# One-hot rows of the sources from TensorE and ScalarE, attention scores from W0 times a, and the batches of the front as straight code

## The reference

```
h = relu(layernorm(x));  hw = h @ W0 + b_w
s_dst = hw @ a[:512];    s_src = hw @ a[512:]
e = leaky_relu(s_dst[dst] + s_src[src] + b_a, 0.2);  w = exp(e)
x = x + segment_sum(w / segment_sum(w, dst)[dst] * hw[src], dst)
h = relu(layernorm(x))
gates = softmax(h @ gate_W + gate_b); top 2 of 4 experts
each expert: 2 times h = relu(mean_of_neighbours(h) @ Wl + bl + h @ Wr)
x = x + sum over the top 2 of gate * expert(h)
```

## Time and profile before

| what | value |
|---|---|
| median of three runs | 859.07 us |
| the profiled execution | 863.82 us, span 862.1 us |
| TensorE, matmuls busy | 752.3 us (87%) |
| VectorE busy | 444.7 us (52%) |
| ScalarE busy | 254.6 us (30%) |
| GpSimd busy | 176.2 us (20%) |
| mean granted TensorE clock | 0.973 |

### The profile page before, as it was taken

How to read it: one execution, slowest core, us unless ns; L and a number is a source line. 1 busy time by engine, 2 the same in 40 slices (tenths; PEclk the granted TensorE clock), 3 DMA queues, 4 the chain that set the end, 5 groups by cost and what they waited for, 6 DMA issues and landing times.

```text
span 862.1 us, 11919 instructions
## 1 busy us (share of the span) xinstructions
PE 752.3 (87%) x3620; PEld 611.0 (71%) x3621; DVE 444.7 (52%) x1088; ACT 254.6 (30%) x516; POOL 176.2 (20%) x160
## 2 busy tenths in 40 slices
PE   1019877499997999998999999989999999999994
PEld 0007655388886888876777777768888888888883
DVE  6999999678876415572263343433223332323230
ACT  0113444555555425141141221312211221212120
POOL 6602433300000001055000000023322332233201
PEclk9999899889997999999999999999999999999997
DMA  4200000011124014769989695369934993449910
GB/s 127 84 0 2 0 0 0 1 59 59 62 84 149 2 49 127 241 195 275 304 285 331 223 348 172 105 197 272 327 94 109 274 330 93 110 108 246 343 22 5
DMA packets 46809, 125.30 MB, mean 145 GB/s; under 512 B 7280, under 2 KB 7412, under 8 KB 46752
## 3 DMA queue, kind: packets, MB, share of 16 engines
q1 hardware_dynamic: 29072, 81.58, 29.0%
q0 software_dynamic: 9232, 26.17, 12.1%
q10 hardware_dynamic: 8448, 16.78, 5.6%
HBM read 72.19 MB, written 53.20 MB: 145 GB/s over the span
## 4 chain that ended last, share of the span: by engine, by line
PE 71%; DVE 18%; DMA 4%; issue 3%; DVEq 1%; ACT 1%; POOL 0%; POOLq 0%; SPq 0%; ACTq 0%
PE ps L1417 15%; PE ps L1419 15%; PE ps L1418 15%; PE ps L1714 6%; PE ps L1713 5%; DVE onehot_g L1025 5%; PE ps L1579 3%; DVE column L1013 3%; PE ps L1580 3%; PE ps L1641 3%; DMA raw<-in_L_gnn_Wr 2%; DVE onehot_p L966 2%; PE ps L1685 1%; PE ps L1724 1%; PE ps L1510 1%
## 5 line engine op out<-in xcount | busy, mean ns | idle before, releaser
L1714 PE MATMUL ps<-slots,CTs 125*128 x230 | 90.9, 395 | 0.0
L1713 PE MATMUL ps<-slots,CTs 125*128 x207 | 81.6, 394 | 0.0
L1345 DVE CAST CTs<-ps 125x512 fp32r<-125x512 f32 (+1 forms) x69 | 37.3, 595 | 85.1 <-PE ps L1641 62.0
L611 POOL DMA_INDIRECT out<-tg,rec x23 | 36.9, 1605 | 192.3 <-ACT tg L877 175.5
L1252 DVE TENSOR_TENSOR he_t<-ps,b_b 125x512 f32<-125x512 f32 x40 | 27.5, 690 | 86.1 <-PE ps L1419 73.8
L1390 DVE TENSOR_TENSOR tm<-ps,b_b 128x512 f32<-128x512 f32 x23 | 15.9, 691 | 102.3 <-PE ps L1419 102.3
L1417 PE MATMUL ps<-W,h2T_hi 128*125 128x512 f32 x160 | 64.2, 401 | 2.8 <-DVE W L1220 2.8
L827 ACT ACTIVATE slots<-he_t 125x512 fp32r<-125x512 f32 x40 | 25.3, 635 | 132.3 <-DVE he_t L1252 113.3
L1418 PE MATMUL ps<-W,h2T_hi 128*125 128x512 f32 x160 | 63.8, 399 | 0.0
L1419 PE MATMUL ps<-W,h2T_lo 128*125 128x512 f32 x160 | 63.7, 398 | 0.0
L1417 PE MATMUL ps<-W,agT_hi 128*125 128x512 f32 x160 | 63.6, 397 | 0.0
(11 more groups left out here) (268 smaller groups left out, 1722.9 us busy)
## 6 DMA issues: line engine op xcount, KB each, us to landing
he_d<-slots SPq DMA_DIRECT2D x30, 448.0 KB
slots<-he_d SPq DMA_DIRECT2D x30, 448.0 KB
w_d<-slots SPq DMA_DIRECT2D x3, 4096.0 KB
slots<-w_d SPq DMA_DIRECT2D x24, 512.0 KB
t_d<-he_t SPq DMA_DIRECT2D x40, 224.0 KB
c_d<-c_nat SPq DMA_DIRECT2D x10, 546.9 KB
raw<-in_L_gnn_Wl ACTq DMA_DIRECT2D x4, 1024.0 KB
raw<-in_L_gnn_Wr ACTq DMA_DIRECT2D x4, 1024.0 KB
```

The costliest lines, as they stand in the source:

```text
L611: g.indirect_dma_start(out, bass.IndirectOffsetOnAxis(ap=i32(rec[:, i, 2:3]), axis=0), tg[i % 3][:], None, bounds_check=N - 1, oob_is_err= ...
L1345: v.tensor_copy(CTs[:, 4 * r:4 * r + n, :], ps[0:P, r, 0:n * S].rearrange("p (c n) -> p c n", n=S)).then_inc(cts_ready.sem, 1)
L1713: mm(o, CTs[:, t, :], part(k, P, t * 1024, P), start=False, stop=False)
L1714: last = mm(o, CTs[:, t, :], part(k, P, t * 1024 + D, P), start=False, stop=t == T - 1)
```

## The change

The edges are laid out as 6 groups of 32 chunks on 32 partitions, the last group padded. `onehot_p` is made by TensorE and ScalarE. With q = source - 125 * tile - 62 and j a place from -62 to 62, TensorE computes 2qj - q^2 + 1 - j^2 = 1 - (q - j)^2 as a product of `e_q` (q, q^2 by ScalarE's Square, and a row of ones) and `q_sel`, and ScalarE's Relu makes zero and one of it (`hot_columns`). One block (`hot_block`) is two matmuls of 500 columns for eight chunks; there are 22, the last of two chunks. Block u uses banks 0 and 1 or 2 and 3 and waits for `hot_ready(u - 1)`. On TensorE's queue stand blocks 0 and 1, the spans' matmul and the transposes of the edge rows, blocks 2 to 6, the table matmuls, blocks 7 to 13, the 16 transposes of W0, blocks 14 to 21, W0 times `a` (16 matmuls) and the sum of `b_w` times `a` (4). VectorE copies the transposed W0 out (4 times), and makes `bw_2`, `W0_lo`, `wa` and `s_add` behind the statistics of x. Scores come from h times (W0 times a): W0 is transposed by TensorE (16 transposes) and multiplied by `a`, giving four columns `wa` (two halves, high and low), and in each batch eight small matmuls take the place of GpSimd's products. The bias `b_w` goes in as a matmul with one row of ones. ScalarE takes the columns of differences from VectorE. In the new `tile_and_batch`, transposes, counts and the `more` code are as before; `turned_high0(b)` and `norm(b + 1)` wait for `turned(b + 1)`, `windows_out(b)` for `batch_done(b + 1)`, `product_low(t)` for `hw_hi_ready(t + 1)` and `turned_low0(b)` for `hT_hi_ready(b + 1)`. The high part of the product is copied from PSUM by ScalarE (`product_high`), the low part is VectorE's (`product_low`). GpSimd only makes constants. W0 and the vectors are loaded from ScalarE's queue. The loops over batches become straight code. The diff, cut to its core:

```diff
@block.sync
-            sp.dma_start(W0_f[:], W0.rearrange("(c k) d -> k c d", k=128)).then_inc(w0_in.sem, 16)
...
+            sp.wait_ge(*pad_ready(1))
...
@block.gpsimd
+            link(g.iota(q_i[:], pattern=[[1, P]], base=-(P // 2), channel_multiplier=0))
...
+            link(g.memset(f32(e_q[2 * CR:, :, :]), 1.0))
+            pool.sem_inc(q_consts.sem, 1)
...
-            g.tensor_tensor(W0_lo[:], W0_f[:], f32(W0_hi[:]), ALU.subtract)
-            with pool.Fori(0, T) as t:
...
@block.scalar
+            act.dma_start(W0_f[:], W0.rearrange("(c k) d -> k c d", k=128)).then_inc(w0_in.sem, 16)
...
+            act.wait_ge(*q_ready(1))
+            a.activation(e_q[CR:2 * CR, :, :], f32(e_q[0:CR, :, :]), ACT.Square).then_inc(square_ready.sem, 1)
+            def hot_columns(u):
+                n = min(CU, NCH - u * CU)
+                act.wait_ge(*hot_made(u + 1))
+                m = min(n, CU // 2)
+                a.activation(onehot_p[:, u * CU:u * CU + n, :].rearrange("p (h c) n -> p h (c n)", c=m),
+                             ps[0:P, u % 2 * 2:u % 2 * 2 + n // m, 0:m * P], ACT.Relu).then_inc(hot_ready.sem, 1)
+            def columns(b):
+                los = first_chunks(act, b)
+                apart(act)
+                if b > 1:
+                    act.wait_ge(*step_ready((b - 1) * BW))
+                for k in range(BW):
+                    last = a.activation(column[:, b % 2 * BW + k, :], e_gc[:, bass.ds(los[k], G)], ACT.Identity,
+                                        bias=wbase[:, b * BW + k:b * BW + k + 1])
+                last.then_inc(column_ready.sem, 1)
+            def product_high(t):
+                act.wait_ge(*hw_done(t + 1))
+                copy(nat_hi[:, t, :], ps[0:P, 6, :]).then_inc(hw_hi_ready.sem, 1)
+            for u in range(NU):
+                hot_columns(u)
+                if u == 1:
+                    act.wait_ge(*rows_turned(1))
+                    copy(e_gc[:], ps[0:P, 7, 0:CG * CR]).then_inc(cols_ready.sem, 1)
+                if u == 9:
+                    act.wait_ge(*w0_in(16))
+                    copy(W0_hi[:], W0_f[:]).then_inc(w0_hi_ready.sem, 1)
...
+                    copy(bw_2[0:1, :], bw_f[:]).then_inc(bw_hi_ready.sem, 1)
+                if u == NU - 6:
+                    act.wait_ge(*tab_ready(1))
+                    columns(0)
+                if u == NU - 4:
+                    act.wait_ge(*var_ready(1))
+                    a.activation(std[:], std[:], ACT.Sqrt).then_inc(std_ready.sem, 1)
+                    act.wait_ge(*norm_ready(1))
+                    norm(0)
+            for b in range(T):
+                turned_high0(b)
+                if b + 1 < T:
+                    norm(b + 1)
+                    columns(b + 1)
+                else:
+                    a.activation(spark[:], spark[:], ACT.Exp)
+                if b > 0:
+                    product_high(b - 1)
+                windows_out(b)
+            row_out(0)
+            product_high(T - 1)
@block.vector
+            v.memset(e_i[:, :, WHOLE, :], 0).then_inc(pad_ready.sem, 1)
+            for k in range(4):
+                c = slice(8 * k, 8 * k + 8)
+                v.tensor_tensor(q_sel[:, c, :], q_row[:].unsqueeze(1).broadcast_to([2 * CR + 1, 8, P]),
+                                q_at[:, c].unsqueeze(2).broadcast_to([2 * CR + 1, 8, P]), ALU.mult
+                                ).then_inc(sel_ready.sem, 1)
+            v.tensor_scalar(e_src[:], e_i[:, 0], -float(P // 2), None, ALU.add)
+            link(v.tensor_scalar(e_t[:], e_i[:, 0], 1.0 / P, -0.496, ALU.mult, ALU.add))
+            link(v.tensor_scalar(e_t[:], e_t[:], MAGIC, MAGIC, ALU.add, ALU.subtract))
+            v.scalar_tensor_tensor(e_q[0:CR, :, :], e_t[:], float(-P), e_src[:], ALU.mult, ALU.add).then_inc(q_ready.sem, 1)
-            for c in range(HR):
-                v.tensor_scalar(onehot_p[:, c, :], iota_h[:, 0:P], e_pg[:, 0, c:c + 1], None, ALU.is_equal)
...
+            def tile_and_batch(b):
+                more = more_here(dve, b)
+                dve.wait_ge(*column_ready(b + 1))
+                for k in range(BW):
+                    if b > 0:
+                        dve.wait_ge(*step_used((b - 1) * BW, k + 1))
+                    for j in range(G):
+                        last = v.tensor_scalar(onehot_g[:, k, j, :], iota_h[:], column[:, b % 2 * BW + k, j:j + 1], None, ALU.is_equal)
+                    last.then_inc(step_ready.sem, 1)
+                    if k == 1 and b > 0:
+                        product_low(b - 1)
+                        if b == T - 1:
+                            source_sums(0, T - 2)
+                    if k == 3:
+                        turned_low0(b)
@block.tensor
...
+            pe.wait_ge(*hot_ready(NU))
+            for b in range(T):
...
+                pe.wait_ge(*hT_lo_ready(b + 1))
+                for c in range(KC):
+                    first = mm(o, hT_hi[:, c], wa[:, c], start=c == 0, stop=False, skip_group_check=True)
+                    last = mm(o, hT_lo[:, c], wa[:, c], start=False, stop=c == KC - 1, skip_group_check=True)
+                last.then_inc(s_done.sem, 1)
+                if b == T - 1:
+                    spread(0)
+                if b > 0:
+                    pe.wait_ge(*hw_lo_ready(b))
+                mm(o, ones_2[:], bw_2[:], start=True, stop=False)
...
```

More of the change, by code:

```diff
@@ L168, in gnn_kernel, with early @@
         W0_f = at("W0_f", [128, KC, D], F32, 34016)
[L169 to L182, removed]
+        o4 = [R5]
+        def early(name, shape, dt):
+            size = 4 if dt != F16 else 2
+            for n in shape[1:]:
+                size *= n
+            t = at(name, shape, dt, o4[0])
+            o4[0] += (size + 31) // 32 * 32
+            return t
+        e_gc = early("e_gc", [P, CG * CR], F32)
+        iota_h = early("iota_h", [P, WT], F16)
+        wbase = early("wbase", [P, NW], F32)
+        tab_x = early("tab_x", [1, NW, 4], I32)
+        tab_b = early("tab_b", [1, T, 8], I32)
+        fl_f = early("fl_f", [1, 2], F32)
+        a_c = early("a_c", [128, 2, KC], F32)
+        bw_c = early("bw_c", [128, KC], F32)
+        ab_c = early("ab_c", [128, KC], F32)
+        wa = early("wa", [128, KC, 4], F32R)
+        s_add = early("s_add", [P, 1], F32)
+        s_part = early("s_part", [P, T, 2], F32)
+        s_both = early("s_both", [P, T, 2], F32)
+        spark = early("spark", [1, 1], F32)
+        bw_f = early("bw_f", [1, D], F32)
+        bw_2 = early("bw_2", [33, D], F32R)
+        ones_2 = early("ones_2", [33, P], F32R)
+        column = early("column", [P, 2 * BW, G], F32)
+        diag = early("diag", [P, 8, P], F32)
+        assert o4[0] <= R5 + 12032
         row_low = at("row_low", [P, N], F32, R2)
@@ L391, in gnn_kernel @@
         QN = N // Q
-        CONSTS = 9
+        CONSTS = 8
         TURNS = (4, 4, 2)
@@ L1448, in count_step, with spread @@
                 return last
-            def tile_and_batch(b):
-                los, more = batch(pe, b)
-                pe.wait_ge(*hT_lo_ready(b, 1, 1))
-                pe.wait_ge(*h_ready(b, 1))
+            def spread(k):
+                pe.wait_ge(*sd_ready(k + 1))
+                n, to = SPREAD[k], 4 * k % 8
+                mm(ps[0:P, SPREAD_BANKS[k], 0:n * P], ones[0:P, 0:P], diag[:, to:to + n, :].rearrange("p a c -> p (a c)"),
+                   start=True, stop=True).then_inc(sd_spread.sem, 1)
+            def tile_and_batch(b):
+                los = first_chunks(pe, b)
+                more = more_here(pe, b)
+                if b > 0:
+                    pe.wait_ge(*hT_lo_ready(b))
+                else:
+                    pe.wait_ge(*wa_ready(2))
+                pe.wait_ge(*h_ready(b + 1))
                 for c in range(KC):
```

424 lines of the change are left out of this document (234 added, 190 removed).

## The result

The changed kernel takes **906.74 us** (median of four runs, 903.5 to 909.21), the kernel before 858.04 in the same comparison (four runs, 856.48 to 866.15). The ratio is 1.054, 95% interval 1.0478 to 1.0602: **slower**, as forecast (900, range 863 to 916). The profiled execution took 903.5 us, its span is 901.8, against 862.1 before: 39.7 us.

What follows compares the result with a forecast made beforehand. VectorE was taken to set the pace in the first 171 us, TensorE after. Terms -2.0 + 44.9 - 2.4 + 0.5 give +41 on the profiled 863.8 us; moved by the same amount, the median 859.07 becomes 900, range 863 to 916.

Steps and rivals of the forecast that it cites:

- The step that decides: The batches, from the second batch's transposes to the tenth's: 121.6 us against 76.7, so 44.9 lost.
- the ring: In each batch TensorE, ScalarE and VectorE wait for one another in written order: 12.1 us at 2.4 GHz, 16.3 at 1.2.
- Its lap: One batch, from the end of its transposes to the end of the next batch's: 15.2 us.
- the weight of the slow clock: In the batches, 15.2 us taken between 12.1 and 16.3, nearer the low end of the clock.
- later stages: The stages from the second layer's first matmul on: 0 us of change.
- the tail: From the last batch's transposes to the first weighted matmul: 20.5 us against 22.9, 2.4 gained; 22 at the low clock.
- The clock: TensorE, idle about 3 us in every batch, has its granted clock at 0.50 in part of most batches.
- The front: Up to the end of the second batch's transposes: near 70 us against 71.9, 2 gained.
- Attention: The last batch's product_low, last diagonal and row_out stand inside the first steps of attention: 0.5 us lost.
- Rival 1: In the batches, the ring with the clock held at 2.4 GHz in most: 12.1 us each, 873 us; chance 0.18.
- Rival 2: In the batches, the ring does not bind and TensorE bounds at 8.2 us each: 841 us; chance 0.10.
- Rival 3: Instruction fetch at TensorE's jump over `more` in each batch: +4 to +8 us over the forecast, 907; chance 0.06.

Runs made afterwards that it cites:

- Experiments 1 and 2: Changed kernel with ScalarE's product_high(b - 1) moved to the batch head: 868.79 us; changed kernel with VectorE's product_low(b - 1) moved behind k4 (batches 1 to 8): 855.75 us.
- experiment 5: Changed kernel with product_high(b - 1) at the batch head, product_low(b - 1) behind k4 (batches 1 to 8) and turned_low0(b) behind k4: 833.88 us.
- experiment 3: Changed kernel with 24 unused 256-column matmuls added on TensorE in each of batches 1 to 8, where it stood idle: 888.99 us.
- Experiment 6: As experiment 5, with the product of W0 and a put between the last blocks of source one-hots on TensorE: 831.28 us.
- experiment 4: Kernel before the change with its four loops over batches written out as straight code, nothing else: 861.98 us, ratio 1.0022.
- experiment 7: As experiment 4, with the five columns of differences made by ScalarE a batch ahead, GpSimd keeping its products: 851.68 us.
- experiment 9: As experiment 4, without GpSimd's offsets and VectorE's comparison, VectorE making all 170 chunks' source one-hots directly: 861.09 us.
- experiments 6 and 8: Experiment 6 as it stands, 831.28 us, and with the last batch's product_high, product_low and spread_out(2) moved later, 823.43 us.

## Why the prediction was right

**The step that decides was right, and so was its mechanism.** The batches are a ring through ScalarE's and VectorE's orders. VectorE's idle time before `product_low`, released by `nat_hi`, is 82.4 us in nine waits, 9.2 each (forecast 6 to 9 us a batch: the laps at the low clock have 10.3 to 10.7); TensorE's before `k2` is 3.6; the clock is 0.50 in part of every batch. Experiments 1 and 2 show the ring by cutting it on either side, experiment 5 by cutting it on both: 66.3 us of 124.8 were nothing but the order of the same instructions and the clock that fell with it.

**Its lap was a little short.** 15.6 us a batch for 15.2. From T(b), forecast and measured:

| mark | forecast, 2.4 GHz | measured, T(1) to T(2), 2.4 GHz from the scores on | measured, T(2) to T(3), 1.2 GHz to near its end |
|---|---|---|---|
| `product_low` ends | 3.1 | 3.5 | 3.5 |
| scores start | 7.6 | 8.2 | 8.2 |
| bias matmul starts | 8.5 | 9.2 | 10.0 |
| transposes end | 12.1 | 13.1 | 16.4 |

Two terms make most of the 1.0 us. The five small `columns` of ScalarE took 1.04 us, put at 0.5: each is 0.2 whatever its five elements. And the bias matmul with the first of the product took 0.42 and 0.34, put at 0.235 each. The counts of `k4`, which ran at 1.2 GHz in both laps, add some 0.2. At 1.2 GHz the ring was put at 16.3 and came to 16.4 to 16.9; that agreement is in part luck, since the same small terms were over and the clock came back before or during the transposes of these laps (0.59 to 0.96 us for the 1.07 put in). My 15.2 was a weighting of 12.1 and 16.3; the run gave two laps at 13.1, one at 15.4 and five at 16.4 to 16.9. So the weight of the slow clock was close and the small operations were dear. The weight itself was a judgement: three dips in nine batches pointed to it, no row gave it.

**The sum is closer than its parts.** +41.0 against +39.7 in the profiled pair owes something to chance: the stages that the forecast added up came to +44.9 (-2.2 + 48.1 - 0.9 - 0.1), and -5.2 of scatter in the later stages, which it put at nothing, hid the difference. Against the medians the forecast of 900 was 6.7 us short: 3.2 of it in the batches and 1.5 in the tail.

**The clock.** The earlier trace rows bore the argument. Before, with 1.4 us idle a batch, three batches of nine dipped; after, with 3.6, all eight did. By the rule that I set against the trace (the Trainium skill, TensorE: Matmul & The Clock Gate, HAM oscillation: a matmul loop with a long wait in each turn restarts slow in every turn) all eight laps would have been slow. The trace agrees: the clock dipped in all eight laps. (Before the change there was a wait in each turn too, and six of nine batches did not dip.) But what a dip costs depends on where it falls. In the laps of 13.1 us (T(1) to T(2), T(6) to T(7)) it was back before the product; of the first of them:

```profile
74.00:76.00 2.00, 1.55 (x8) 1.33 (x9) 2.00 (x9) 0.00 (x0) 0.00 (x0) 0.67 0.01 4
76.00:78.00 2.00, 1.78 (x10) 1.34 (x8) 2.00 (x11) 0.00 (x0) 0.00 (x0) 0.50 0.00 0
78.00:80.00 2.00, 2.00 (x14) 1.65 (x13) 0.68 (x4) 1.47 (x5) 0.00 (x0) 0.98 0.04 8
```

There it ran over `k2` to `k4`, which VectorE paces, and cost next to nothing: experiment 3's laps without a dip are 12.9 to 13.1. Experiment 3 gave back 16.0 us in the batches and 3.5 in the tail. By its laps without a dip the clock is about 21 of the 48.1 us lost in the batches, the ring's length at full clock 27.

**The front came as summed, by cancelling terms.** The lines that answer to the earlier trace rows:

```profile
5.24 4.77 DVE L974 TENSOR_TENSOR q_sel<-q_row,q_at 65x1000 fp32r<-65x1000 f32 x4 [4.04 <-POOLq L557]
...
14.88 1.90 ACT L687 ACTIVATE onehot_p<-ps 125x1000 bf16<-125x1000 f32 x2 [1.28 <-PE ps L1510]
...
18.25 0.32 DVE L998 SCALAR_TENSOR_TENSOR g_c<-g_it,g_hit 50x170 f32<-50x170 f32 x1
...
46.71 2.14 ACT L687 ACTIVATE onehot_p<-ps 125x1000 bf16<-125x1000 f32 x3
...
48.11 6.83 PE L1549 MATMUL ps<-a_c,W_t 128*128 128x2 f32 x32
```

`q_sel` cost 4 x 1.19 (put at 1.15), the first Relu began at 14.9 (14.3), the blocks ended at 48.9 (50), the 40 small passes took 48.3 to 56.6 (8.4 forecast, 8.3 measured). The operation that took 3.9 us took 0.32. T(0) came 1.4 us early (57.97 for 59.4), and T(1) is 69.75 for 70 because the first batch took 11.8 us for 10.6. Experiment 6 shows that about half of the small passes' 8.3 us could be covered: T(0) came 4.1 us earlier there.

**The tail** was put at 20.5 and took 22.0. 22.0 is what I had worked out for a tail wholly at the low clock, and 20.5 was a choice between that and 17.9; the clock was at 1.2 GHz until 211 us, through all of the scores and nearly all of the product. Experiment 3, with the clock held, had 18.5, experiment 5 15.3.

**Attention** lost nothing (95.8 us for 95.9): the moved pieces cost no time that shows, and the 0.5 was spare.

**The rivals.** Rival 1 (clock held) did not happen. Experiment 3 comes nearest to it: 889, not 873, because the ring at 2.4 GHz is 13.0 and not 12.1 and three laps still took 14.6. Rival 2 (the ring does not bind, TensorE does) did not happen either: VectorE stood idle 7 to 10.7 us a batch for `nat_hi`. Experiment 5 reaches what it describes by another order, and there 8.2 us a batch is too high; the load is 7.3, since 25 counts take 2.6 us when nothing paces them and not 3.3. Rival 3 (instruction fetch): experiment 4 puts straight code at +0.2% with an interval that holds zero, and after the change, at the place of the jump, in front of the scores, there is one issue gap of 0.2 us in ten batches. The 906.74 is its number (907) by coincidence: most of the excess over 900 lies in the terms named above. By the Trainium skill (Runtime: NRT & Kernel Launch, Instruction fetch mechanics) the jumps over `more` could have cost a fetch each; no run here shows such a stall.

**What the change itself brings** is thus two things of opposite sign. Its moves of work, in the right order, are worth 3% (experiment 5, ratio 0.9688); the order it put them in costs 9% on top (906.74 against 833.88). Taking VectorE's held instructions away (experiment 7) or GpSimd's load off at one place (experiment 9) is worth little: 1% and nothing that can be told, for the hold lands on the VectorE instruction that stands there instead. By the Trainium skill (SBUF — State Buffer, Who interferes with whom) a VectorE instruction that reads two SBUF inputs contends with a GpSimd instruction that reads SBUF, and one in a two-port mode with any of GpSimd's; whichever issues first locks the other out for the whole instruction. The traces agree in the size of the hold: 4.3 us over for GpSimd's 4.53. Which mode the one-hots run in, they do not show. Only with GpSimd's arithmetic gone altogether does VectorE have both: 25 one-hots in 5.0 us (4.97 in experiment 4 too) and nothing held beside them.

**Open.** Why the clock came back at 78 us, before the product, in one lap and only at 98 in the next, though TensorE idled 3.61 us in both. And where the 8 us between the medians of experiments 6 and 8 lie: 2 are seen at the first weighted matmul, the rest is in no trace. Nor was `turned_low0` moved by itself, so its share of experiment 5 is not known.

## What to carry to other kernels

Before a load sum is believed, walk each engine's written order and ask for each wait what stands in front of the signal it waits for on the other engine; here three operations of 0.6 to 0.7 us in the wrong place (`product_high`, `product_low`, `turned_low0`) cost 66 us with no engine full. If TensorE is in such a ring, its idle time can be paid twice, since work behind it then runs at half clock, as in six of eight laps here. And a GpSimd instruction that holds VectorE costs it most of its own length (4.3 us for 4.53, 2.8 for three of 1.3), whatever stands there; moving the victim away saved 1.0 us of 3.7 a batch.

## What the runs showed of the hardware

- Filling TensorE's idle time with 24 useless matmuls a batch made the kernel 18 us faster (888.99 for 906.74).
- TensorE at 1.2 GHz, matmuls of two and four columns: 0.21 us from one to the next; the four-column ones at 2.4 GHz 0.11. For so few columns the clock halves the rate too, so W0 times `a` (32 passes, 6.8 us) is dear for its handful of columns.
- Five ScalarE operations on 125 x 5 elements took 1.04 us (84.08 above), nearly twice the 0.58 of one copy of 125 x 512: small work is priced by the instruction.
- The same batch, the same instructions: 16.4 us and 7.3 us.
